# First layer of a four-layer graph network: filter index on the partitions, one-hot tile in f32 that carries the squared edge value

## The reference

```
h  = softplus(einsum('bijg,fg->bijf', g, W1) + b1) - ln 2
Wf = einsum('bijf,gf->bijg', h, W2) + b2
rf = einsum('bjd,fd->bjf', r, Wa)
Am = A[:, :, :, None]
Wf = Wf * Am
y  = einsum('bjf,bijf->bif', rf, Wf * Am)
y  = ssp(einsum('bif,df->bid', y, Wd1) + bd1)
y  = einsum('bid,ed->bie', y, Wd2) + bd2
```

## Time and profile before

| | us |
|---|---|
| median of three runs | 1770.27 |
| profiled execution | 1770.88 |
| its span, first to last instruction | 1768.7 |
| TensorE matmul busy | 1375.5 (78%) |
| VectorE busy | 1176.1 (66%) |
| ScalarE busy | 807.2 (46%) |
| GpSimd busy | 741.7 (42%) |

### The profile page before, as it was taken

The page is one execution under the profiler, slowest core; times in us unless marked ns, Lnnn a source line. Parts: engine busy times, 40 slices in busy tenths (PEclk is TensorE's granted clock), DMA queues, the critical chain, the costliest instruction groups (busy, mean ns, idle before and its releaser), DMA issues. The chain is left out here.

```text
span 1768.7 us, 37607 instructions
## 1 busy us (share of the span) xinstructions
PE 1375.5 (78%) x8705; PEld 1125.1 (64%) x8736; DVE 1176.1 (66%) x5246; ACT 807.2 (46%) x1921; POOL 741.7 (42%) x1378
## 2 busy tenths in 40 slices
PE   4888888888888888888854756666666788888884
PEld 3777777777777777777743545455455565555563
DVE  5777777777777777777624888888887333333337
ACT  2656565656555655556521223222232233333347
POOL 4455445544554445544533655656655100000007
PEclk9999999999999999999975688787788899999989
DMA  3332233323332333223300000000000000000003
GB/s 88 85 82 75 74 77 87 76 71 80 81 80 74 75 85 81 71 76 82 77 3 19 25 13 24 21 14 24 12 30 13 1 1 0 0 0 0 0 0 96
DMA packets 140443, 82.82 MB, mean 47 GB/s; under 512 B 64963, under 2 KB 136031, under 8 KB 140385
## 3 DMA queue, kind: packets, MB, share of 16 engines
q1 hardware_dynamic: 138660, 81.06, 17.6%
q10 hardware_dynamic: 1725, 1.13, 0.2%
HBM read 77.31 MB, written 4.82 MB: 46 GB/s over the span
## 5 line engine op out<-in xcount | busy, mean ns | idle before, releaser
L715 PEld LDWEIGHTS wf<-w2t,hid 128*128 128x128 f32 x1536 | 351.4, 315 | 36.0 <-issue 36.0
L715 PE MATMUL wf<-w2t,hid 128*128 128x128 f32 x1536 | 371.7, 396 | 0.0
L904 DVE SCALAR_TENSOR_TENSOR msg<-wf,val_sq,rfe 128x128 f32<-128x128 f32 x768 | 210.3, 343 | 177.4 <-PE wf L715 145.5
L604 ACT ACTIVATE rfe<-rg 128x768 f32<-128x768 f32 x128 | 102.7, 803 | 210.6 <-PE rg L731 210.6
L510 POOL TENSOR_TENSOR xb<-xin,bd2bc 128x128 f32<-128x128 f32 x64 | 29.2, 457 | 397.3 <-DVE xres L894 397.0
L731 PE MATMUL rg<-rf_hi,pick 128*128 128x128 bf16 x768 | 155.5, 237 | 10.3 <-issue 9.1
L731 PE MATMUL rg<-rf_mid,pick 128*128 128x128 bf16 x768 | 155.2, 237 | 0.0
L731 PE MATMUL rg<-rf_lo,pick 128*128 128x128 bf16 x768 | 154.0, 235 | 0.0
L1634 POOL MEMSET r_minus_half<- 128x4 f32 x1 | 0.1, 102 | 328.0 <-POOLq L1504 328.0
L1530 PEld LDWEIGHTS r_zgi<-xin,w_hh 128*128 128x128 f32 x508 | 67.0, 192 | 98.6 <-issue 87.7
L1582 DVE SCALAR_TENSOR_TENSOR r_new<-r_gates 128x64 f32<-128x64 f32 x128 | 28.8, 225 | 148.2 <-ACT r_gates L1563 148.2
(11 more groups left out here) (282 smaller groups left out, 3696.9 us busy)
## 6 DMA issues: line engine op xcount, KB each, us to landing
val_bc<-edge_val SPq DMA_DIRECT2D x256, 96.0 KB, 2.7
idx_bc<-edge_idx SPq DMA_DIRECT2D x128, 192.0 KB, 3.0
adj_w<-in_adj_rows SPq DMA_DIRECT2D x64, 64.0 KB, 2.4
xt_w<-in_x_cols SPq DMA_DIRECT2D x64, 64.0 KB, 2.0
adjt_w<-in_adj_t SPq DMA_DIRECT2D x64, 64.0 KB, 1.9
xin<-in_x_rows SPq DMA_DIRECT2D x32, 128.0 KB, 2.1
m_adj_g<-in_adj_rows SPq DMA_DIRECT2D x16, 256.0 KB, 2.8
m_adjt_g<-in_adj_t SPq DMA_DIRECT2D x16, 256.0 KB, 2.8
```

What stands on the lines that cost most here:

```text
L604: act.activation(rfe[:, q, :].rearrange("p (a n) -> p a n", a=2), rg[:, :, 0:HALF], ACT.Copy).then_inc(s["rfe_ready"], 1)
L715: last = pe.matmul(column(wf, r), h[:, r, :], w2t[:, :], start=True, stop=True)
L904: last = dve.scalar_tensor_tensor(msg[:, q, r * P:(r + 1) * P], column(wf, r), val_sq[:, q4, r:r + 1], rfe[:, q, r * P:(r + 1) * P], ALU.m ...
```

## The change

wf is made with W2 as the stationary operand and h streaming, two f32 products of 384 columns, so the filter index is on the partitions and the 768 edges are in the columns. The gathering is turned the same way: rf in f32 is stationary, and the one-hot tile streams, in f32. The one-hot tile carries the squared edge value, which comes by a new DRAM array, edge_sq, loaded to all partitions (sq_bc) in place of val_own. b2 is a column that VectorE adds in the message operation, so the b2 part with the transposed adjacency falls away, and so do the three bf16 parts of rf. GpSimd's sums now end in y itself. The indices are cast to bf16 by ScalarE and squared values made by GpSimd. The overflow column is multiplied with Wd1 first (over_u) and placed by a second product into p_u. The smallest entry of the adjacency is found by ScalarE.

```diff
         def load_unit(u, d, g, dg, kk):
...
-                sp.dma_start(val_own[:, q, :],
-                             val_src[bass.ds(gi, 1), kk, :, :].rearrange("a i r -> (a i) r")).then_inc(unit_in[q], 16)
+                sp.dma_start(sq_bc[:, q, :], sq_src[bass.ds(gi, 1), kk, :, :].rearrange("a i r -> a (i r)")
+                             .broadcast_to((P, UNIT))).then_inc(unit_in[q], 16)
...
                         w(sp, "edges16", g.at(2) + 1)
+                        w(sp, "squares_ready", g.at(2) + 1)
...
+                        for dst, src in ((edge_val, found[:, q, 0:2 * R]), (edge_sq, squares[:, q, :]),
+                                         (edge_idx, ei16[:, q, :])):
+                            sp.dma_start(dst[bass.ds(g.at(2), 1), :, :, :].rearrange("a h i r -> (a i) h r"),
+                                         src.rearrange("p (h r) -> p h r", h=2)).then_inc(edges_stored, 16)
+                        sp.wait_ge(edges_stored, 48 * (g.at(2) + 1))
```

The order of the work on ScalarE (k_in = 0 is the first unit of a graph; the lines for the Square, the two exponentials and the logarithm between them stay):

```diff
                         w(act, "rg_ready", u.at() + u0 + 1)
                         after(act, "msg_ready", u, -2, u0)
+                        act.activation(halves(rfe[:, u.mod(2), :]), rg[:, :, 0:HALF], ACT.Copy)\
+                            .then_inc(s["rfe_ready"], 1)
+                    if k_in == 0 and g.has(-2):
+                        w(act, "uclamped_ready", g.at(-2) + g0 + 1)
+                        act.activation(t_ex[:, :], t_cl[:, :], ACT.Exp).then_inc(s["uexp_ready"], 1)
+                        w(act, "uexp_ready", g.at(-2) + g0 + 1)
+                        act.activation(t_lg[:, :], t_ex[:, :], ACT.Ln, bias=1.0).then_inc(s["ulog_ready"], 1)
                     if u.has(2):
...
+                    if not dense and k_in == 0 and g.has(-1):
+                        w(act, "over_u_p", g.at(-1) + 1)
+                        after(act, "u_ready", g, -2, 0)
+                        act.activation(over_u[:, :], p_over_u, ACT.Copy).then_inc(s["over_u_ready"], 1)
                     if k_in == 0 and g.has(1):
                         w(act, "rf_ready", g.at(1) + g0 + 1)
                         after_graph(act, g, -1, "rg_ready")
-                        after(act, "rfb_ready", g, 0, g0)
-                        act.activation(rf32[:, :], p_rf, ACT.Copy)
-                        act.activation(rf_hi[:, g.mod(2, 1), :], p_rf, ACT.Copy).then_inc(s["rfhi_ready"], 1)
+                        act.activation(rf32[:, g.mod(2, 1), :], p_rf, ACT.Copy).then_inc(s["rfhi_ready"], 1)
+                    if not dense and k_in == 0 and g.has(2):
+                        q = g.mod(2, 2)
+                        w(act, "picks_ready", g.at(2) + 1)
+                        if not g.static or g.at(2) >= 2:
+                            act.wait_ge(edges_stored, 48 * (g.at(2) - 1))
+                        act.activation(ei16[:, q, :], found[:, q, RANKS:RANKS + 2 * R], ACT.Copy)\
+                            .then_inc(s["edges16"], 1)
```

ScalarE then takes the adjacency's least entry (minus, with a sum). TensorE and VectorE:

```diff
-                        for r in range(R):
-                            last = pe.matmul(column(wf, r), h[:, r, :], w2t[:, :], start=True, stop=True)
+                        for half in range(2):
+                            last = pe.matmul(wf[:, half, 0:HALF], w2t[:, :], hid[:, q, half * HALF:(half + 1) * HALF],
+                                             start=True, stop=True)
...
+                        for half in range(2):
+                            picked = pick[:, u.mod(2, 1), half * HALF:(half + 1) * HALF]
+                            last = pe.matmul(rg[:, half, 0:HALF], rf32[:, gn.mod(2), :], picked,
+                                             start=True, stop=True)
...
+                        if not dense and g.has(-1):
+                            w(pe, "over_u_ready", g.at(-1) + 1)
                         after(pe, "rfhi_ready", g, 0, g0)
                         pe.matmul(p_rf, xt_w[:, qg, :], wat[:, :], start=True, stop=True).then_inc(s["rf_ready"], 1)
...
+                        dve.scalar_tensor_tensor(pick[:, u.mod(2, 1), :], idx_bc[:, q4, :], iota_col[:, :],
+                                                 sq_bc[:, q4, :], ALU.is_equal, ALU.mult)\
+                            .then_inc(s["pick_ready"], 1)
...
+                        dve.scalar_tensor_tensor(halves(msg[:, q, :]), wf[:, :, 0:HALF], b2c[:, :],
+                                                 halves(rfe[:, q, :]), ALU.add, ALU.mult)\
+                            .then_inc(s["msg_ready"], 1)
```

GpSimd (the view m takes every sixth element, so the six edges of a node stand 24 bytes apart):

```diff
+                        m = msg[:, q, :].rearrange("p (i r) -> p r i", r=R)
+                        wide = 3 if dense or k_in == 0 else 2
+                        rest = sum1[:, 2, :] if wide == 3 else m[:, 4, :]
+                        total = y[:, g.mod(2), :]
+                        pool.tensor_tensor(sum1[:, 0:wide, :], m[:, 0:wide, :], m[:, wide:2 * wide, :], ALU.add)\
+                            .then_inc(s["sum1_ready"], 1)
```

More of the change, by code:

```diff
@@ L288, in layer0 @@
     rg = ps("rg", [P, 2, 512])
-    yp = ps("yp", [P, 512])
+    ub = ps("ub", [P, 512])
     mb = ps("mb", [P, 512])
-    p_out = rg[:, 0, HALF:512]
-    p_u = rg[:, 1, HALF:512]
+    p_out, p_u = ub[:, 0:P], ub[:, P:2 * P]
+    p_over_u = mb[:, 2 * P:3 * P]
+    p_b2 = mb[:, 203:204]
     p_rf = mb[:, 0:P]
@@ L511, in body @@
                             .then_inc(s["xb_ready"], 1)
[L512 to L548, removed]
-                            pool.tensor_tensor(sum4[:, :], sum3[:, 0, :], sum3[:, 1, :], ALU.add)\
-                                .then_inc(s["sum4_ready"], 1)
@@ L700, in body @@
                             .then_inc(s["z_ready"], 1)
-                    if k_in == 1 and g.has(-1):
-                        w(pe, "yt_ready", g.at(-1) + g0 + 1)
-                        after(pe, "rfe_ready", u, 0, u0)
-                        pe.matmul(p_u, wd1t[:, :], yt[:, :], start=True, stop=True).then_inc(s["u_ready"], 1)
-                    if k_in == 1 and g.has(-2):
-                        w(pe, "uh_ready", g.at(-2) + g0 + 1)
-                        after(pe, "rfe_ready", u, 0, u0)
-                        pe.matmul(p_out, t_h[:, :], wd2t[:, :], start=True, stop=True).then_inc(s["out_ready"], 1)
+                    if not dense and k_in == 1 and g.has(3):
+                        w(pe, "cnt", g.at(3) + 1)
+                        if g.has(1):
+                            w(pe, "rfhi_ready", g.at(1) + 1)
+                        pe.matmul(p_start, before[:, :], over_cnt[:, :], start=True, stop=True)\
+                            .then_inc(s["start_ready"], 1)
                     if u.has(0):
@@ L767, in body @@
-                    if not dense and k_in == 0 and g.has(3):
-                        w(pe, "cnt", g.at(3) + 1)
-                        if g.has(1):
-                            w(pe, "rfhi_ready", g.at(1) + 1)
-                        pe.matmul(p_start, before[:, :], over_cnt[:, :], start=True, stop=True)\
-                            .then_inc(s["start_ready"], 1)
+                    if k_in == 0 and g.has(-2):
+                        w(pe, "uh_ready", g.at(-2) + g0 + 1)
+                        pe.matmul(p_out, t_h[:, :], wd2t[:, :], start=True, stop=True).then_inc(s["out_ready"], 1)
@@ L787, in _ @@
                 dve.tensor_scalar(before[:, :], iota_row[:, :], iota_col[:, :], None, ALU.is_gt)
-                dve.tensor_copy(found[:, 2 * RANKS + 1:], iota_col[:, :]).then_inc(ident_ready, 1)
+                for q in range(2):
+                    last = dve.tensor_copy(found[:, q, 2 * RANKS + 1:], iota_col[:, :])
+                last.then_inc(ident_ready, 1)
             def rank_edges(g):
@@ L903, in body @@
-                        for r in range(R):
-                            last = dve.scalar_tensor_tensor(
-                                msg[:, q, r * P:(r + 1) * P], column(wf, r), val_sq[:, q4, r:r + 1],
-                                rfe[:, q, r * P:(r + 1) * P], ALU.mult, ALU.mult)
-                        last.then_inc(s["msg_ready"], 1)
+                        after(dve, "sum3_ready", u, -2, u0)
+                        if not dense and k_in == 1:
+                            after(dve, "over_u_p", g, -1, 0)
@@ L917, in body @@
-                        dve.tensor_tensor(t_h[:, :], t_u[:, :], t_lg[:, :], ALU.max).then_inc(s["uh_ready"], 1)
+                        dve.scalar_tensor_tensor(t_h[:, :], p_u, bd1c[:, :], t_lg[:, :], ALU.add, ALU.max)\
+                            .then_inc(s["uh_ready"], 1)
+                    if not dense and k_in == 0 and g.has(3):
+                        rank_edges(g)
                     if dense and u.has(1):
```

271 lines of the change are left out of this document (114 added, 157 removed).

## The result

The changed kernel takes 2010.78 us in the median (2004.53 to 2012.88) against 1770.37 for the kernel before, run beside it: ratio 1.135, 95% interval 1.133 to 1.138. The forecast was 1800, at most 1850. The direction was right, the size was not: +240 us instead of +30. All of it lies in the first layer.

The account below looks back on a forecast made before the run. TensorE was taken to set the pace before, a closed chain through ScalarE's cast after: 63 turns of 14.16 us give +39, the tail -3 and -5, so +31 on 1771, called 1800 us, range 1750 to 1850.

Parts of the forecast that it names:

- the y wait: TensorE's wait for ScalarE's copy of y, 103.5 us in 57 times, 1.8 each, expected to go.
- msg and pick: VectorE's two operations of 768 elements, put near 1.0 us each; their changes of -0.6 and +0.5 cancel.
- GpSimd's strided sum: GpSimd's first sum, reading every sixth element: the sums grow by about 0.9 us, hidden behind other engines.
- The wait that decides: Closed loop, one turn a graph: ScalarE's Square, index cast, stores, landing, loads, next graph's Square; 14.16 us a turn.
- The tail: After the last store: -3 us to the Square that uses it, -5 from there to the layer's end.
- the chain's length: One turn from Square to Square, summed from rows: 14.16 us, from 13.4 to 15.3.
- The last store to the first load: SyncE's wait until its stores have landed, from the last store's issue to the first load: 2.82 us.
- The squares' landing: DMA of 384 KB of squares to all partitions, from issue to arrival: 3.6 us, between 2.8 and 4.7.
- The path from Square to cast: ScalarE's queue from Square through Exp, Exp, Ln, over_u and rf32 to the index cast's end: 4.33 us.
- Rival C: TensorE idles several us a graph and its clock falls: turn 14.6 to 15.0 us, about 1840 us, chance 0.15.
- Rivals A and B: A: squares land in 2.8 to 3.0 us, 1757 us, chance 0.16. B: chain doesn't close, 1628 us, chance 0.14.
- B's limit: SyncE's own serial work with the landing, next to set the pace if the chain doesn't close: 11.4 us a graph.

Follow-up runs that it names:

- e1: The changed kernel with the cast of the indices to bf16 back on VectorE, right after the overflow pick: 1750.46 us, ratio 0.989 to the kernel before.
- e5: The changed kernel with the cast still on ScalarE but ahead of the Square of the same step: 1756.02 us, ratio 0.991 to the kernel before.
- e2: The changed kernel with the edge values' loads on their own semaphore, the only one ScalarE's Square waits for: 1755.04 us, ratio 0.991 to the kernel before.
- e3: The changed kernel without the third store, sq_bc loaded from the values instead of their squares: 1901.92 us, ratio 1.074 to the kernel before.
- e4: The changed kernel with 3 KB of squares loaded per unit instead of 384 KB to all partitions: 1849.03 us, ratio 1.044 to the kernel before.
- e6: The changed kernel with 3 KB of squares for each graph's second unit only, the first keeping 384 KB: 1967.85 us, ratio 1.112 to the kernel before.

## Why the prediction was off

- That TensorE sets the pace before, and that the y wait and the yp products go: as written. Two products of wf take 1.4 us at a granted clock of 1.00 (518.11 to the next start at 519.50), two of rg 1.46 to their modelled end, not 1.7:

```profile
518.11 1.56 PE L695 MATMUL wf<-hid,w2t 128*128 128x384 f32 x4
519.50 0.49 PE L704 MATMUL mb<-wd1t,msg 128*128 128x128 f32 x2
519.83 1.46 PE L725 MATMUL rg<-pick,rf 128*128 128x384 f32 x4
```

- msg and pick "near 1.0" each: 1.018 and 1.025. GpSimd's strided sum stayed hidden.

```profile
L856 DVE SCALAR_TENSOR_TENSOR msg<-wf,b2c,rfe 128x768 f32<-128x768 f32 x128 | 130.3, 1018 | 173.5 <-PE wf L695 173.5
...
L835 DVE SCALAR_TENSOR_TENSOR pick<-idx_bc,iota_col,sq_bc 128x768 f32<-128x768 bf16 x128 | 131.2, 1025 | 27.6 <-DMA sq_bc<-edge_sq 27.4
```

- The wait that decides, its order and its place: right. e1 and e5 open the chain at two places, e2 shortens it by 3.5 us of landing and more, and each gives back 255 to 260 us.
- The tail was right by luck: -8 forecast, -8.6 measured, from two misses that cancel. From the last store to the Square that uses it 13.3 us passed, where 9.6 was forecast and 12.7 was before; from there to the layer's end 24.2, where 28.4 was forecast and 33.4 was before.
- The step that failed is the chain's length, 14.16 against 17.52, three terms of it. The last store to the first load was read from one graph, 2.82, where the mean before is 3.33 (-0.51), and taken as unchanged, while the third store adds 0.98 (e3) and the squares in flight about 0.45 (e4, e6, which overlap with it in part): 1.72 in all. The squares' landing was put at 3.6 by the fastest row in sight, a stretch of another layer at 350 GB/s; to the Square it is 5.05, against 3.66 (1.39 more), and beyond even the bound of 4.7. It is made up of 3.05 for a 3 KB load (2.8 was again one graph's), 1.81 for the size, where 0.8 was forecast, 0.14 for the second unit's traffic and the wake-up. The formula of the Trainium skill, DMA: Bandwidth & Descriptors, Anatomy of one DMA, that the prediction quotes with 2.9 us, is fitted there to DMAs that GpSimd issues. These go out from SyncE, and the trace doesn't agree with it: 5.0. The path from Square to cast was 0.33 longer, as p_rf mostly came at the low clock (its own terms add up to 4.36, not 4.33).
- That makes 3.36 us a turn above the forecast. With 63 turns it is 212 us, against 211 missed. Cast to first store and first to fourth load were exact (0.01, 0.00), and the three stores took 0.09 less than forecast.
- Rival C: the clock fell to 0.79, but of the chain it accounts only for the 0.33. In order of time, TensorE's p_rf after its wait of 6.01 took 0.79 instead of 0.44. The granted clock was 0.50 from 508.0 to 509.2, and TensorE had run no matmul from 505.0 to 508.0:

```profile
508.31 0.79 PE L737 MATMUL mb<-wat,xt_w 128*128 128x128 f32 x2 [6.01 <-ACT over_u L620]
```

- Rivals A and B didn't come. B's limit, SyncE's serial queue, was put at 11.4 and turned out at about 12.4 once the chain was opened (e1). The stores' landing there is 4.59 instead of 2.82.
- The bounds of the sum, 13.4 to 15.3, come from one link alone, the squares' landing; the stores' landing got none. But every link is paid 63 times, 0.5 us of doubt in a turn is 32 us, and three links were wrong to the same side.

## What to carry to other kernels

When a small operation moves to another engine, look for what stands ahead of it in that queue, and whether one of those waits for what the moved operation releases: then queue order closes a loop, and every link of it, down to DMA landings, is paid in full each turn. A sum of its links proves nothing, since it always gives the turn; look for slack in each. Price such a loop with means over many turns and with the slowest row for a landing, not with one graph and the best rate. A semaphore that counts transfers an engine doesn't read puts them in its path.

## What the hardware showed that was not expected

- In the graph shown, the index store lands 4.2 us after its issue, and no packet starts in 2.5 us of it that the window covers (share and GB/s at the end of the row, both 0). So most of this landing isn't spent in moving the core's own bytes; what it is spent on, no run here shows. Traffic still counts for some of it: e4 and e6 load fewer bytes and come 0.44 and 0.48 sooner to the first load. In the kernel before the landing of the index store was 2.9 in the median, in the changed kernel 4.1.

```profile
512.50:515.00 2.50, 2.50 (x7) 1.59 (x7) 0.66 (x2) 1.04 (x2) 0.00 (x0) 0.50 0.00 0
```

- GpSimd's sum with reads 24 bytes apart costs 1282 against 1009 ns for 384 columns and 878 against 788 for 256: 27% and 11%, less than the half that the Trainium skill, GPSIMD Engine Reference, Performance pitfalls for Q7 kernels, gives and the prediction quotes.

```profile
L501 POOL TENSOR_TENSOR sum<-msg 128x384 f32<-128x384 f32 x57 | 73.1, 1282 | 28.5 <-DVE msg L856 28.5
...
L501 POOL TENSOR_TENSOR sum<-msg 128x256 f32<-128x256 f32 x57 | 50.0, 878 | 605.1 <-DVE msg L856 605.1
```

The kernel before:

```profile
L533 POOL TENSOR_TENSOR sum<-msg 128x384 f32<-128x384 f32 x57 | 57.5, 1009 | 0.0
...
L533 POOL TENSOR_TENSOR sum<-msg 128x256 f32<-128x256 f32 x56 | 44.2, 788 | 0.0
```
